# Products without a reader, made by TensorE while it waits at the beginnings of six stages

## The reference, cut to what matters

```python
x = x + _layernorm(_L0_attn_ref(_layernorm(x), ...))   # 16 heads of 16, softmax(q k^T) v, rotary positions
x = x + _layernorm(_L1_ffn_ref(_layernorm(x), ...))    # 16 experts, the best 2 for each token, and a shared one
x = x + _layernorm(_L2_attn_ref(_layernorm(x), ...))   # h = dA * h + dBx over the tokens; y = sum(h * C)
x = x + _layernorm(_L2_ffn_ref(_layernorm(x), ...))    # gate and up, then two layers of 1024 x 1024
x = x + _layernorm(_L3_attn_ref(_layernorm(x), ...))   # as the first, with a position bias added to the scores
```

## Time and profile before

| | us |
|---|---|
| median of 3 runs | 4319.74 |
| the profiled execution | 4321.57 |
| its span | 4319.8 |
| TensorE busy in the span | 3980.5 (92%) |
| VectorE busy | 3322.9 (77%) |
| ScalarE busy | 2849.1 (66%) |
| GpSimd busy | 2003.2 (46%) |
| mean granted clock of TensorE | 0.963 |

### The profile page before, as it was taken

How to read it: one execution, slowest core, us unless ns; L and a number is a source line. 1 busy time by engine, 2 the same in 40 slices (tenths; PEclk the granted TensorE clock), 3 DMA queues, 4 the chain that set the end, 5 groups by cost and what they waited for, 6 DMA issues and landing times. The chain is left out here.

```text
span 4319.8 us, 100821 instructions
## 1 busy us (share of the span) xinstructions
PE 3980.5 (92%) x39417; PEld 2123.1 (49%) x39417; DVE 3322.9 (77%) x5680; ACT 2849.1 (66%) x4554; POOL 2003.2 (46%) x1898
## 2 busy tenths in 40 slices
PE   8899999988959757899999999999999999999897
PEld 4344444564538423354544445455454555555555
DVE  7899999686665569888888888886137888888586
ACT  5577777664553155888888888875125777777664
POOL 5222222251235635888888888886001222222332
PEclk9899999998979979899999999999998999999999
DMA  4211111105335345455565655654223222222100
GB/s 146 66 39 39 39 39 39 27 28 124 73 114 160 98 113 125 125 156 160 148 169 146 149 146 156 170 151 134 87 90 106 65 65 61 61 70 61 31 13 27
DMA packets 263805, 412.40 MB, mean 95 GB/s; under 512 B 52731, under 2 KB 139802, under 8 KB 263170
## 3 DMA queue, kind: packets, MB, share of 16 engines
q1 hardware_dynamic: 228966, 375.81, 32.1%
q0 software_dynamic: 6912, 18.88, 1.8%
q10 hardware_dynamic: 27456, 11.28, 1.2%
HBM read 351.85 MB, written 53.24 MB: 94 GB/s over the span
## 5 line engine op out<-in xcount | busy, mean ns | idle before, releaser
L2968 POOL TENSOR_TENSOR l_dbx<-l_u,l_bc 128x1024 f32<-128x1024 f32 x256 | 603.4, 2357 | 247.3 <-DVE banks L3489 84.3
L1169 DVE CUSTOM_DVE_ANT_0 banks<-banks,l3s_table 128x1024 f32<-128x1024 f32 x512 | 619.4, 1241 | 89.5 <-PE banks L1089 84.7
L1252 ACT ACTIVATE l3s_probs<-banks 128x512 f32<-128x512 f32 x1024 | 540.3, 595 | 204.1 <-PE banks L1118 100.8
L1164 DVE TENSOR_REDUCE l0s_peak<-banks 128x1 f32<-128x1024 f32 x512 | 605.3, 1214 | 58.3 <-PE banks L1089 57.9
L1252 ACT ACTIVATE l0s_probs<-banks 128x512 f32<-128x512 f32 x1024 | 535.7, 600 | 164.8 <-PE banks L1089 163.1
L3276 ACT ACTIVATE banks<-l_dt,l_decay 128x512 f32<-128x512 f32 x512 | 346.7, 687 | 221.6 <-DVE banks L3489 219.1
L2978 POOL TENSOR_TENSOR l_ys<-l_ys,l_hc 128x1024 f32<-128x1024 f32 x203 | 479.6, 2362 | 21.5 <-DVE l_hc L3500 21.4
L3150 PE MATMUL banks<-l_ha,l_ring 128*128 128x512 f32 x1024 | 446.6, 593 | 3.9 <-issue 3.9
L3150 PE MATMUL banks<-l_hb,l_ring 128*128 128x512 f32 x1024 | 443.1, 593 | 1.6 <-ACT l_hb L3241 0.8
L3489 DVE TENSOR_TENSOR_SCAN banks<-banks,l_carry,l_dbx 128x512 f32<-128x512 f32 x256 | 319.3, 1279 | 68.7 <-ACT banks L3276 61.8
L1089 PE MATMUL banks<-l3s_q_st,l3s_k_st 122*32 122x512 bf16 x4096 | 346.9, 381 | 4.8 <-ACT l3s_probs L1252 1.0
(11 more groups left out here) (531 smaller groups left out, 7166.9 us busy)
## 6 DMA issues: line engine op xcount, KB each, us to landing
l_bc<-l_bc_rows SPq DMA_DIRECT2D x256, 512.0 KB, 5.4
l_ring<-in_l2f_stream SPq DMA_DIRECT2D x176, 512.0 KB, 6.4
l3s_table<-bias_table SPq DMA_DIRECT2D x16, 960.0 KB
qk_parts<-l0s_probs SPq DMA_DIRECT2D x96, 128.0 KB, 2.4
qk_parts<-l3s_probs SPq DMA_DIRECT2D x32, 384.0 KB, 3.5
y_rows<-l1f_out_b SPq DMA_DIRECT2D x80, 128.0 KB, 1.7
l0s_q_st<-qk_parts SPq DMA_DIRECT2D x64, 96.0 KB
l0s_k_st<-qk_parts SPq DMA_DIRECT2D x64, 96.0 KB
```

The source lines that it names most:

```text
L1164: nc.vector.tensor_reduce(out=peak[:, b % 2, t:t + 1], in_=s1[t % 2], axis=AX, op=ALU.max, negate=True).then_inc(s1_used, 1)
L1169: nc.vector.tensor_tensor_reduce(out=s1[t % 2], in0=s1[t % 2], in1=rows, scale=1.0, scalar=LOW, op0=ALU.add, op1=ALU.max, accum_out=peak[: ...
L1252: nc.scalar.activation(columns(probs[b % 2][:, t, :], half * 512, (half + 1) * 512), scores, ACT.Exp, scale=scale).then_inc(s2_used, 1)
L2968: nc.gpsimd.tensor_tensor(dbx[:, at:at + 2], u[:, 2 * mh:2 * mh + 2], bc[:, load % BR, 0].unsqueeze(1).to_broadcast([P, 2, TB]), ALU.mult)\
```

## The change

At six places TensorE is given products whose result nobody reads. Each writes to a bank that TensorE owns at that moment and that it overwrites next. (1, 2) In both attentions, after each tile of pass1 in the steps without pass2: four more quarter products, 14 times. (3) In the experts, 6 products of identity by 512 columns of float32, before the wait for the owners. (4) At the start of the scan, 3 such products, before the first transposes. (5) In the scan's n = 1, 8 of them before outputs(0, 0). (6) In n = 1, 24 of them before the wait for rows_l_ready.

```diff
@@ attention_core, TensorE, step @@
                     elif job:
                         pass1(*job)
+                    if job and "2" not in passes:
+                        in_quarters(s2[slot // 2 % 2], k_st[job[1] % BATCH][0:STACK, 0:P],
+                                    moving(q_st[job[1] % BATCH], STACK, 0), start=True, stop=True)
@@ mixture, TensorE @@
+            for _ in range(6):
+                nc.tensor.matmul(PS[:, 2, :], chip.ident[:], acc[:, 0:2, :].rearrange("p k d -> p (k d)"), start=True, stop=True)
             pe.wait_ge(owner_ready, 16)
@@ scan_and_mlp, TensorE @@
+            def warm(group, products):
+
+                bank = bank_for(pe, group)
+                for _ in range(products):
+                    nc.tensor.matmul(banks[:, bank, :], chip.ident[:], chip.x[:, 0:2, :].rearrange("p k d -> p (k d)"),
+                                     start=True, stop=True)
...
+            warm("turn0.0", 3)
             for c in range(KC):
                 turn_rows(0, c)
...
+                if n == 1:
+                    warm("y0.0", 8)
                 if 0 <= b < NB:
                     for i in range(2):
                         outputs(b, i)
...
+                if n == 1:
+                    warm("turn_l0.0", 24)
                 if 0 <= b < NB:
                     pe.wait_ge(rows_l_ready, n)
```

## The result

The changed kernel takes 4341.15 us (median of 5 runs, 4334.49 to 4346.91) against 4319.74 (the median of the kernel before, over five runs too): the ratio is 1.0042, with a 95% interval of 1.0031 to 1.0053, which is 13 to 23 us slower. The forecast was 4339.8 in a range of 4331 to 4347.

The account below looks back on a forecast made before the run. TensorE was taken to bound the layers from 1762 us, so later entry is paid in full. Places 6, 5, attentions, 3 and 4 summed 19.4 + 1.9 - 1.4 + 0.2 + 0 = +20.1 us: 4339.8 us, range 4331 to 4347.

Parts of the forecast that it names:

- The bound: Layers from 1762 to 3280 us: TensorE busy 1489.18 of 1518 us, so each microsecond it enters later is one at the end.
- the cold share: Place 6: extra time for added products run before the clock rises, 0.8 us, with 0 and 2 as ends.
- +1.9 us passes on to place 6: Place 5: ScalarE's 1.9 us wait reaches VectorE's statistics and the norm, moving place 6's beginning by the same.
- The part with pass2: Attentions once pass2 joins: a high clock can save only VectorE's waits for scores, 0.9 and 1.15 us.
- 0.1 us a tile lost until the clock rises: Attentions, pass1: three groups a tile take 1.28 us against VectorE's 1.18 at the low clock, some 0.3 us lost.
- VectorE sets the pace: Attentions, steps with pass1 alone: VectorE busy 3.96 of 4 us, TensorE 3.42, so VectorE determines 1.18 us a tile.
- the balance of 2.9 us late against 2.7 us warm: Place 3, experts: products end 2.9 us late, the high clock from the first block saves 2.7, net +0.2.
- neither ... gets through: Place 4, scan's start: neither a 2 us delay nor a faster clock reaches ScalarE or VectorE, 0 us.
- Catching up: Rival at place 6: other engines get ahead, TensorE's 2.50 and 5.14 us waits vanish; +12.5 us, 4332.2, chance 0.08.
- The cheap product: Rival at places 5 and 6: a product costs a quarter, at most +3.3 us less 1.4; 4321.6, chance 0.03.
- the change is not done: Rival: unread products are dropped or a place is not reached; 4319.7 us, chance 0.05.
- The side of faster: Rival: place 6 fits the 12.57 us idle time or rows_l_ready comes only at 1763; -9.55 us, 4310.2, chance 0.04.

## Why the prediction was right, and where it was not

**The bound, and place 6.** That a microsecond before 1762 us is a microsecond at the end holds: from the first record of hidden(0, 0) to the last attention it is 1502.6 us before, 1504.0 in the changed kernel, 1501.7 with place 6 alone and 1502.9 with 48 products (1501.7 to 1505.5 over all traces). The price per product (0.87 put, 0.82 to 0.86 measured), its place behind project_dt and the stall of the scan were as put. The sum was +19.4, measured +21.3 with place 6 alone and +21.9 in the changed kernel, just above its upper end of 21. Most of the miss is in the cold share: 0.8 us were put, with 2 as the upper end, and the products show 1.5 to 3.0. It was a guess as well: by the premise, 4 us at half speed from the start of project_dt on, 0.3 us were left for the added products. That premise is what failed. The clock had not begun to rise with project_dt's records; in the changed kernel it was still 0.50 in the first of these windows:

```profile
1744.00:1748.00 4.00, 4.00 (x6) 1.34 (x5) 4.00 (x7) 3.32 (x7) 4.00 (x2) 0.50 0.17 43
1748.00:1752.00 4.00, 4.00 (x8) 1.70 (x7) 2.29 (x7) 0.00 (x0) 3.86 (x5) 0.68 0.17 65
```

A second part was not in the sum at all. Counted from the start of project_dt, the changed kernel is later by 21.7 us at the transposes (20.1 put), by 20.8 at the first record of L3149, and by 20.3 behind TensorE's next wait: up to there 1.4 us are given back, where 0.7 were put. Then it loses 1.5 again. TensorE waits 6.22 us, the granted clock falls back to 0.50, and the next 48 records take 23.87 us, where they took 22.33 before:

```profile
1759.88 22.33 PE L3137 MATMUL banks<-l_xtl,l_ring 128*128 128x512 f32 x48 [5.14 <-issue]
```

```profile
1785.42 23.87 PE L3149 MATMUL banks<-l_xtl,l_ring 128*128 128x512 f32 x48 [6.22 <-issue]
```

```profile
1780.00:1784.00 4.00, 0.00 (x0) 0.00 (x0) 2.47 (x3) 3.98 (x8) 4.00 (x3) 0.66 0.41 129
1784.00:1788.00 4.00, 2.58 (x3) 1.18 (x4) 2.64 (x4) 1.89 (x3) 3.08 (x2) 0.50 0.50 117
1788.00:1792.00 4.00, 4.00 (x7) 1.58 (x6) 1.72 (x2) 3.92 (x4) 2.34 (x1) 0.56 0.00 0
```

So the clock that 24 products had raised was back at 0.50 by 1784 us, 15 us after the last of them. How many records behind that wait run at the low clock differs from kernel to kernel, 2 to 6 of them, also where nothing is added there; this is the 1.6 us of scatter in dt to hidden.

**Place 5.** +1.9 was put, +0.3 measured. ScalarE did wait as put (2.04 us against 1.9), and VectorE's statistics came 2.15 us later. The step that failed is "+1.9 us passes on to place 6": the next reader, GpSimd, was not waiting for the statistics, its queue was behind. The row that says so (L2978 until 1723.2) stood in the trace of before, and I had followed the wait only as far as VectorE.

**Places 1 and 2.** -1.4 was put for both together, with -2.1 as the lower end; -1.7 and -2.6, in sum -4.3, were measured. The part with pass2 is nearly as put: from the 15th maximum to pass3, 1.1 and 1.3 us are saved, 2.4 where 2.05 were put. The step that failed is the cost in pass1, "0.1 us a tile lost until the clock rises": the 14 tiles became shorter, by 0.6 us in the first attention and 1.3 in the second. A maximum that follows a wait takes 1.23 us, and before they followed each other at 1.18; at the high clock they follow at 1.14 (9.10 us for 8):

```profile
138.21 9.10 DVE L1167 TENSOR_REDUCE l0s_peak<-banks 128x1 f32<-128x1024 f32 x8
```

In the second attention VectorE was not without gaps in pass1 at the low clock: 14 tiles took 18.25 us before and 16.93 after. One window of before, and one of the changed kernel:

```profile
3292.00:3296.00 4.00, 3.35 (x32) 0.41 (x24) 3.76 (x7) 0.00 (x0) 0.00 (x0) 0.50 1.03 353
```

```profile
3324.00:3328.00 4.00, 2.95 (x48) 0.75 (x40) 4.00 (x7) 0.00 (x0) 0.86 (x4) 1.00 0.35 122
```

"VectorE sets the pace" was read off the first attention and not looked up in the second.

**Place 3.** +0.2 was put; 139.7 to 140.2 us with the 6 products, 139.7 to 141.0 without. Zero within the scatter, and the balance of 2.9 us late against 2.7 us warm is in the traces: in the changed kernel the first block begins 7.1 us after the numbering instead of 4.3, and its turn_hidden after 10.15 us instead of 10.45. The 2.8 us are made up within the first block.

**Place 4.** 0 was put, -1.3 measured. The failed step is "neither ... gets through": I looked at who waits for the first projections and not at the end of TensorE's unbroken row, where ScalarE waits.

**The sum.** By local stretches the pair gives 21.9 + 0.3 - 1.7 - 2.6 - 0.2 - 1.3 = +16.4 us, where +20.1 was forecast and the runs show 13 to 23. The misses partly cancel: place 6 dearer by 2.5, place 5 cheaper by 1.6, the gains of the attentions and of place 4 larger by 4.2, place 3 by 0.4. That the median of +21.4 is so near to the forecast is in part luck. The 5 us between it and +16.4 are in none of these stretches, and are not explained.

**The rivals.** Catching up is refuted (with 24 products the wait behind place 6 grew, and the cost rises evenly to 48). The cheap product is refuted for float32 and shown for bfloat16: 6.60 us for 24. The Trainium skill's 0.216 us for a warm product of 512 columns ("TensorE: Matmul & The Clock Gate", "Back-to-back issue gap", there the gap of an isolated product) agrees with these records, which follow each other at 0.216 us, and not with a float32 product, whose two records take 0.858. That the change is not done is refuted by 70 records of L3055, 35 products. The side of faster fell at 1741.60, as put.

## What to carry to other kernels

A product made only to keep the clock high is work like any other: count its records by type, and compare them with the wait that is left at its exact place in the engine's list, not with the largest idle time nearby. Where it fits it gained here (1.7, 2.6 and 1.3 us in local stretches, in no total), and 24 of them in bfloat16 gave the same clock in 28% of the time of float32. What it buys lasts only until the next long wait. Before a delay is put on the path, follow it to each next reader and ask whether that one was waiting at all; a busy queue in between can swallow it up to its own lag and nothing beyond.

## What the runs showed of the hardware

The clock granted to TensorE stayed at 0.50 for the whole of pass1 with the engine busy for 3.42 of 4 us, was raised with four more quarter products a tile (0.84 in 128 to 132 us, 1.00 in the three windows after), and fell back to 0.50 within 8 us when they stopped after 6 tiles. In the scan it fell from 1.00 to 0.50 in a wait of TensorE of 6.22 us. So keeping it high took the added products to the end of the phase, not just to its first rise.

Untouched stretches wander more than most edits here are worth: from the end of the first attention to the experts' routing it took 384.8 to 397.9 us over the traces of this study, and its length follows no edit. The one kernel that was traced twice had the same length within 0.5 us both times, on two chips, so that the length may belong to the kernel rather than to the run; no other kernel was traced twice. A change of 5 us in this kernel is seen in local stretches of the trace, and not in the total.
